# Splitting message rows: the two subtractions go from GpSimd to VectorE

## The reference

```python
xn = _layernorm(x)
x = x + L0_gnn(xn, src, dst, edge_weight) + L0_mix(xn)      # layer 0
x = x + L0_ffn(_layernorm(x))                               # top-1 of 8 experts
xn = _layernorm(x)
x = x + L1_gnn(xn, src, dst) + L1_mix(xn)                   # layer 1
x = x + L1_ffn(x)                                           # top-2 of 8 experts

def L1_gnn(h, weight, bias, src, dst):
    norm_src = rsqrt(clip(out_degree(src), 1.0))
    norm_dst = rsqrt(clip(in_degree(dst), 1.0))
    msg = (h * norm_src[:, None])[src]
    agg = segment_sum(msg, dst) * norm_dst[:, None]
    return elu(agg @ weight + bias)
```

## Time and profile before

| what | value |
|---|---|
| runs, median (lowest to highest) | 2986.62 us (2985.55 to 2993.79) |
| the profiled execution's own time | 2994.02 us |
| its span | 2992.4 us |
| TensorE busy | 2385.0 us, 80% of the span |
| VectorE busy | 1159.4 us, 39% |
| ScalarE busy | 1103.8 us, 37% |
| GpSimd busy | 542.8 us, 18% |
| mean granted TensorE clock | 0.872 |

### The profile page before, as it was taken

The page is one execution under the profiler, slowest core; times in us unless marked ns, Lnnn a source line. Parts: engine busy times, 40 slices in busy tenths (PEclk is TensorE's granted clock), DMA queues, the critical chain, the costliest instruction groups (busy, mean ns, idle before and its releaser), DMA issues.

```text
span 2992.4 us, 40601 instructions
## 1 busy us (share of the span) xinstructions
PE 2385.0 (80%) x12530; PEld 1931.1 (65%) x12531; DVE 1159.4 (39%) x2546; ACT 1103.8 (37%) x2058; POOL 542.8 (18%) x470
## 2 busy tenths in 40 slices
PE   0777699989889889896679936888788887846887
PEld 0444588877777768775568834666666666635776
DVE  4444577754554544542100034332423334231111
ACT  3122477756555645561223333212222121112232
POOL 1520011100010100102122223010202021113454
PEclk9878799999888898997689977998798897867999
DMA  3321111110110110203332234331222223423443
GB/s 122 95 84 51 30 39 40 44 60 25 34 59 31 53 39 16 75 15 103 101 97 66 64 99 133 95 105 44 75 64 53 71 48 88 122 62 70 82 85 64
DMA packets 163999, 202.07 MB, mean 68 GB/s; under 512 B 55840, under 2 KB 134159, under 8 KB 163860
## 3 DMA queue, kind: packets, MB, share of 16 engines
q0 software_dynamic: 69408, 81.85, 11.8%
q1 hardware_dynamic: 82874, 107.64, 10.9%
q10 hardware_dynamic: 11578, 10.82, 1.1%
HBM read 108.51 MB, written 93.74 MB: 68 GB/s over the span
## 4 chain that ended last, share of the span: by engine, by line
PE 46%; DMA 35%; another core or an unknown queue 7%; ACT 3%; DVE 3%; issue 2%; SPq 2%; POOL 1%; ACTq 0%; DVEq 0%; POOLq 0%
PE bank L738 43%; DMA agg_rows<-agg_t 32%; PE bank L744 3%; POOL w_adj L583 1%; DMA arena<-agg_rows 1%; SPq L411 1%; DMA arena<-in_x 1%; ACT w_qc L1200 0%; DMA xg<-expert_rows 0%; ACT count_a L1200 0%; DMA feat<-row_hot 0%; ACT agg_t L1217 0%; DVE arena L1922 0%; ACT w_adj L1199 0%
## 5 line engine op out<-in xcount | busy, mean ns | idle before, releaser
L738 PE MATMUL bank<-xg,w_adj 125*125 125x256 f32 (+1 forms) x2500 | 583.8, 345 | 1.1 <-DMA w_adj<-counts 1.1
L738 PEld LDWEIGHTS bank<-arena,row_hot 128*125 128x125 f32 x3200 | 428.2, 200 | 87.9 <-issue 67.5
L738 PE MATMUL bank<-arena,row_hot 128*125 128x100 f32 x3200 | 435.6, 283 | 46.9 <-remote 19.6
L738 PEld LDWEIGHTS bank<-xg,w_adj 125*125 125x125 f32 (+1 forms) x2500 | 376.2, 169 | 24.7 <-DMA w_adj<-counts 1.3
L744 PE MATMUL bank<-ident,arena 125*128 125x125 f32 (+1 forms) x650 | 148.3, 355 | 304.2 <-remote 126.3
L738 PE MATMUL bank<-t,w_h 128*128 128x250 f32 (+1 forms) x1184 | 332.5, 435 | 24.4 <-remote 20.3
L744 PEld LDWEIGHTS bank<-ident,arena 125*128 125x128 f32 (+1 forms) x650 | 89.0, 175 | 358.0 <-issue 352.8
L1199 ACT ACTIVATE w_adj<-bank 125x200 f32<-125x200 f32 x400 | 217.3, 543 | 274.6 <-PE bank L738 266.2
L1603 DVE TENSOR_TENSOR row_hot<-iota_all,arena 128x2000 f32<-128x2000 f32 x100 | 223.8, 2238 | 233.7 <-PE bank L738 230.8
L738 PEld LDWEIGHTS bank<-t,w_h 128*128 128x128 f32 x1184 | 234.2, 203 | 120.0 <-issue 68.4
L738 PE MATMUL bank<-w_adj,arena 128*125 128x256 f32 x1024 | 239.9, 392 | 0.0
(11 more groups left out here) (330 smaller groups left out, 3021.2 us busy)
## 6 DMA issues: line engine op xcount, KB each, us to landing
w_adj<-counts POOLq DMA_DIRECT2D x25, 781.2 KB, 8.8
arena<-sorted_in SPq DMA_DIRECT2D x49, 251.0 KB
counts<-count_a SPq DMA_DIRECT2D x13, 781.2 KB
counts<-w_qc SPq DMA_DIRECT2D x12, 781.2 KB
arena<-rows_b SPq DMA_DIRECT2D x5, 1875.0 KB
w_adj<-in_L_ffn_Wd POOLq DMA_DIRECT2D x8, 1024.0 KB, 6.4
w_adj<-in_L_ffn_W POOLq DMA_DIRECT2D x16, 512.0 KB, 5.7
sorted_in<-pad_rows POOLq DMA_DIRECT2D x8, 878.4 KB, 16.8
```

What stands on the lines that cost most here:

```text
L738: return pe.matmul(o, w, r, start=first, stop=last, skip_group_check=not check)
```

## The change

GpSimd keeps only the cast to `part1` (and the column of ones). VectorE makes `rest(s)` one step behind the nodes and `part2(s)` two steps behind: after `nodes1(s)` it makes the rest of step s-1 and the low part of step s-2. The rest of step 4 and the low parts of steps 3 and 4 are made in the first projection, which is taken out of the loop for that, behind its bank reads. `rest` has two buffers now, the second in `count_a`. ScalarE waits for the rest of two steps ago, where it waited for the parts. Two semaphores are new: `rest_made` (VectorE to GpSimd and ScalarE) and `mid_made` (GpSimd to VectorE); `parts_made` now comes from VectorE.

```diff
--- before.py
+++ after.py
@@ -190,7 +190,7 @@
         part0, part1 = parts[:, :, 0:D + 1], parts[:, :, D + 2:2 * D + 2]
         stage_all = row_hot[0:B, :, :, :].rearrange("p k j n -> p (k j n)")
         stage = [stage_all[:, G * D * k:G * D * k + G * D].rearrange("p (i d) -> p i d", i=G) for k in range(2)]
-        rest = stage_all[:, 2 * G * D:3 * G * D].rearrange("p (i d) -> p i d", i=G)
+        rest = [t.rearrange("p (i d) -> p i d", i=G) for t in (stage_all[:, 2 * G * D:3 * G * D], count_a[0:B, 0:G * D])]
         near_i = w_adj[0:B, 0:NB * B].bitcast(I32).rearrange("p (b e) -> p b e", e=B)
         near_f = w_adj[0:B, NB * 128:NB * 128 + NB * B].rearrange("p (b e) -> p b e", e=B)
         seen = [w_adj[0:B, 960 * g:960 * g + 960].rearrange("p (i a k) -> p i a k", i=G, a=3) for g in range(NS)]
@@ -340,6 +340,7 @@
         fout_full, fout_free = sem("f_out_full"), sem("f_out_stored")
         nodes_full, nodes_stored, head_stored = sem("nodes1_full"), sem("nodes1_stored"), sem("nodes1_head_stored")
         msg_full, msg_stored, parts_made = sem("messages1_full"), pair("messages1_stored"), sem("message_parts_made")
+        rest_made, mid_made = sem("message_rests_made"), sem("message_middles_made")
         step_got = [sem(f"step_rows_loaded{s}") for s in range(NS)]
         aggs_used = sem("step_aggs_used")
         last_begun, pads_stored = sem("last_step_begun"), sem("pad_rows1_stored")
@@ -609,12 +610,10 @@
             def message_parts(s):
 
                 at = slice(G * s, G * s + G)
-                pool.wait_ge(msg_full, s + 1)
+                pool.wait_ge(rest_made, s + 1)
                 pool.memset(part0[:, at, D:D + 1], 1.0)
-                chain(pool.tensor_tensor(rest, stage[s % 2], part0[:, at, 0:D], ALU.subtract))
-                chain(pool.tensor_copy(part1[:, at, :], rest))
-                chain(pool.tensor_tensor(part2[:, at, :], rest, part1[:, at, :], ALU.subtract))
-                pool.sem_inc(parts_made, 1)
+                chain(pool.tensor_copy(part1[:, at, :], rest[s % 2]))
+                pool.sem_inc(mid_made, 1)
                 chain.restart()
 
             def gather(layer, b, feat, before):
@@ -1347,7 +1346,7 @@
                 chain(last)
                 if s >= 2:
                     act.wait_ge(msg_stored[s % 2], 16 * (s // 2))
-                    act.wait_ge(parts_made, s - 1)
+                    act.wait_ge(rest_made, s - 1)
                 for i in range(G):
                     b = G * s + i
                     last = act.activation(stage[s % 2][:, i, :], n_big[:, b, :], ACT.Copy, scale=inv_out[:, b:b + 1])
@@ -1974,6 +1973,19 @@
                 dve.sem_inc(nodes_full, 1)
                 chain.restart()
 
+            def rests(s):
+
+                dve.wait_ge(msg_full, s + 1)
+                chain(tt(rest[s % 2], stage[s % 2], part0[:, G * s:G * s + G, 0:D], ALU.subtract))
+                dve.sem_inc(rest_made, 1)
+
+            def lows(s):
+
+                at = slice(G * s, G * s + G)
+                dve.wait_ge(mid_made, s + 1)
+                chain(tt(part2[:, at, :], rest[s % 2], part1[:, at, :], ALU.subtract))
+                dve.sem_inc(parts_made, 1)
+
             def project1(s):
 
 
@@ -1989,6 +2001,10 @@
                         last.then_inc(y_free[i % 2], 1)
                 chain(last)
                 dve.sem_inc(y_free[0], 1)
+                if isinstance(s, int) and s == 0:
+                    rests(NS - 1)
+                    lows(NS - 2)
+                    lows(NS - 1)
 
                 for n in (1, 0):
                     chain(ts(ek[:, :, D * n:D * n + D], row_a[:, :, D * n:D * n + D], 0.0, None, ALU.min))
@@ -2019,9 +2035,15 @@
             dve.sem_inc(k4_used, 1)
             for s in range(NS):
                 nodes1(s)
+                if s >= 1:
+                    rests(s - 1)
+                if s >= 2:
+                    lows(s - 2)
+                chain.restart()
 
             dve.wait_ge(head_stored, 48)
-            with dve.Fori(0, NS - 1) as s:
+            project1(0)
+            with dve.Fori(1, NS - 1) as s:
                 project1(s)
             dve.wait_ge(nodes_stored, 32)
             dve.sem_inc(rowb_used, 1)
```

## The result

| kernel | median of runs | lowest to highest | ratio to before, 95% interval |
|---|---|---|---|
| before | 2988.51 us (20 runs) | 2979.3 to 3001.97 | |
| changed | 3006.37 us (20 runs) | 2993.05 to 3014.57 | 1.0044 [1.0032, 1.0056] |

The ratio is +13.1 us on 2988.51 us, between 9.6 and 16.7 us. The plain medians differ by more, 17.9 us, and the means by 15.8 us; the ratio on record is what is used here. Either way the change makes the kernel slower, by more than the 0.3% that this kernel can tell from nothing.

What follows compares the result with a forecast made beforehand. Stores on the SP queue were taken to bound the message stage, TensorE the time from 1820 us on. Late tail 9.8, queries' wait -1.0, clock 0.5: +9.3 us, 2995.9 us from the median 2986.6; range 2987.5 to 3003.5, forecast's own 2993 to 2999.

Steps and rivals of the forecast that it cites:

- Stores bound the message stage; GpSimd's relief is worth nothing.: Message stage: stores on the SP queue set its length; the 3 us VectorE gains from GpSimd's relief is booked at zero.
- 2.07 us throughout: Message stage, a sign to look for: VectorE's five node instructions take 2.07 us, no longer 5.11 us where GpSimd disturbed them.
- Three instructions behind the bank reads, sums open 7.0 us late.: First projection: VectorE's last rest and two low parts, with GpSimd's cast, make TensorE open the first aggregation 7.0 us late.
- So the tail ends the wait, 10.1 or 8.6 us late: Block 0's first aggregation: tail rows, gathered behind GpSimd's cast, land after TensorE wants them; 9.8 us booked.
- a second pause of 1 to 3 us: Ahead of block 0's tail: TensorE stands a second time, 1 to 3 us, ended by a DMA.
- up to 2 us, which its tail covers: Clock in block 0's aggregation: the first new pause slows it by this much, hidden by the late tail.
- The queries' wait hidden, -1.0 us.: Step 2 of the projection: TensorE's 1.01 us wait behind VectorE's wait for the queries' store disappears, giving back 1.0 us.
- Later waits ... shift with them.: Behind the projection: later waits hang on TensorE and VectorE and merely shift with them; no further cost booked.
- the one that had the low parts alone (+6.6 us): First aggregation: cast goes first, gather lands in 4.2 us, only the low parts count; 2993.2 us, chance 0.18.
- the absorbed case: Aggregation loop: if stores of the aggregates pace it, the next landing eats the late start; 0 to +2 us, chance 0.12.
- The faster case: Message stage: stores land earlier, 4.9 us come back, low parts and tail slip in front of TensorE; 2981.7 us, chance 0.08.
- The worse case: Block 0's tail: load of the edges lands in 6.0 us, gather in 8.7; +15.0 us, 3001.6 us, chance 0.12.

Runs made afterwards that it cites:

- e4: Kernel before with a third staging buffer for the messages, GpSimd's subtractions still in place: 2987.13 us, ratio 0.9998.
- e2: Changed kernel with GpSimd fetching edges and rows of block 0's tail ahead of the cast of step 4: 3001.31 us, one run.
- e1: Changed kernel with VectorE's three late instructions moved ahead of the first projection's bank reads, into its idle time: 2994.33 us, ratio 1.0025.
- e8: e1 with the loop over the projections kept as before, nothing unrolled: 2982.61 us, ratio 0.9998.
- e9: Kernel before with 74 signals that nobody waits for, on VectorE ahead of the mixer loop: 2991.04 us, ratio 1.0012.
- e11: e1 with 181 signals that nobody waits for on VectorE, shifting the mixer loop's head to instruction 2056: 2988.78 us, ratio 1.0013.
- e11b: e1 with 181 such signals split over two waits of VectorE (84 and 97), better hidden: 2986.54 us, ratio 1.0006.
- e10b: Changed kernel with 182 signals that nobody waits for, split over two waits of VectorE (84 and 98): 2996.86 us, ratio 1.0039.
- e10: Changed kernel with 182 signals that nobody waits for, all in one place on VectorE ahead of the mixer loop: 2989.91 us, ratio 1.0026.
- e3: Changed kernel with only the low part of step 4 left behind the bank reads, the other two instructions ahead of them: 3005.95 us, one run.

## Why the prediction came out as it did

The forecast was +9.3 us and the measurement is +13.1. On the median that the prediction started from, 2986.62 us, the ratio gives 2999.8 us: inside the range of 2987.5 to 3003.5 us, just outside the forecast's own 2993 to 2999 us. The sign and the place were right; two steps behind them were not.

- **Stores bound the message stage; GpSimd's relief is worth nothing.** Right. The last message ends at +40.95 and +40.85, and e4 moves it by 5.7 us with a buffer alone. But the node instructions did not go to 2.07 us throughout: the cast is still there and disturbs them, 2.7 to 3.0 us.
- **Three instructions behind the bank reads, sums open 7.0 us late.** Right: 1.49 us each, +6.96 us. The cast was second and took 2.59 us.
- **"So the tail ends the wait, 10.1 or 8.6 us late", with a second pause of 1 to 3 us.** The size was right (10.3 us against 9.8 us), its cause half, and so the close size is partly luck. The pause was 0.37 us, because the working let TensorE want the tail 8.72 us behind the opening, at the higher clock. It wanted it 11.7 us behind, and e2 shows that it would have been as late with the tail there in time. The clock was booked as "up to 2 us, which its tail covers" and 0.5 us behind it; it costs 3.0 to 3.4 us inside the aggregation and is covered only because the tail comes at the same moment.
- **The queries' wait hidden, -1.0 us.** The mechanism is right: VectorE's wait there is 2.17 us and not 13.65, and TensorE's wait behind it is gone.

```profile
1876.94 1.49 DVE L2019 SCALAR_TENSOR_TENSOR count_a<-arena 125x1280 f32<-125x1280 f32 x1 [2.17 <-remote]
```

  The size is not sure. From the second aggregate to the third it takes 30.58 us and not 31.86, 1.3 us less. But in the five other traces whose sums open as early as before (e1, e8, e9, e11, e11b) VectorE waits 12.4 to 13.0 us there, and the interval is 30.56 to 31.27 us. Against those the gain is 0 to 0.7 us.
- **"Later waits ... shift with them."** This is the step that failed: for what comes behind the projection the prediction took a mere shift. It costed each instruction that was added and moved, but not that the projection taken out of its loop makes the stream longer, and its own sum has no term for the fetch. In the profiled executions the three jumps cost 6.8 us by the fourth turn (changed kernel against e10b, and e1 against e11b) and 4.2 us at the end in both pairs. In the timed runs the pairs that differ in little else give 0.05, 0.19 and 0.12% (changed against e10b, e1 against e11b, e9 against before), 3.6 us in the mean, none of them certain alone; by the plain means of the runs the same pairs give 0.25, 0.23 and 0.21%, 6.9 us.

So 10.3 us at the first aggregate, less 0 to 1.3, and some 4 us from the jumps: 13 to 14 us, about what was measured. That sum is only one way to split the loss. It rests on profiled executions, and in these the end is 9.2 us late, because in the last part, the experts, differences of some us come and go. The ends of the traces suggest another split: +1213.0 to +1216.6 in four with neither cause (before, e4, e8, e11b), +1220.5 and +1220.6 with the late opening alone (e10, e10b), +1220.7 and +1222.8 with the jumps alone (e1, e9). (e11 has neither cause but ends at +1220.6; its signals hold the mixer back by 4.8 us.) By these the late opening is worth some 6 us at the end and the jumps some 7. Both causes are shown, the place by e1 against the changed kernel, the jumps by e9 and e10b in both directions; how the 13 us divide between them, 4 to 7 us for the jumps, is an estimate. Of the rivals, the one that had the low parts alone (+6.6 us) falls, since e3 and the clock show that a late opening costs more than itself; the absorbed case falls with e10b, in which the late opening is all that is left and the time is still 0.39% up (0.26% in e10). The faster case falls because the stage did not end sooner. The worse case has the measured size, but not its mechanism: the load of the edges took 4.55 us and the tail's product started 5.4 us behind the gather's issue, no slow landings.

## What to carry to other kernels

A change that moves work must be costed at three places: the instruction's own, the clock of the engine that it lets stand (a pause of 2.4 us added 1.6 us, one of 6.7 us some 3 us), and the length of the stream ahead of loops that come later (three jumps of 2.7 to 3.1 us here). Before unrolling, look at the packets of the instruction queue and at the idle time behind a loop's jump; a few dozen instructions more or less ahead of a long loop can decide it. A start that is made sooner gains only as far as the next fixed event, here a store behind 31.6 us of loads on the same queue.

## What the runs showed of the hardware that was not expected

- A jump back over a loop of some 280 instructions on VectorE took 0.22 to 0.27 us with the loop's first instruction at number 1800, 1825 or 2055, and 2.7 to 3.1 us at 1874, with 8 KB packets of instructions right behind it: 81 in all (82 in e3), against 65 to 67.
- A signal without a wait took VectorE's sequencer 93 to 97 ns: 74 in a row 6.8 us in e9, 182 in a row 17.5 us in e10.
- GpSimd's cast over 1280 elements a row, started 0.01 us behind an fp32 subtraction of VectorE, took 2.59 us and not 1.25 us, which is 0.15 us less than one behind the other (1.49 + 1.25).
